# The opening of a two-layer graph network on one Trainium2 core: norms split, roundings reordered and low parts moved between engines in its first two steps

## The reference, cut to what matters

```
h  = relu(layernorm(x))
m  = Be * (H^T h)                 # Be = 1 / column counts
u  = H m ;  z = (u W1^T) * Dn + b1        # Dn = 1 / (H w), a guarded inverse
n  = layernorm(relu(z)) * gamma + beta
g  = Be * (H^T (n W2^T)) ;  x1 = x + h + Dn * (H g) + b2
xl = relu(layernorm(x1))
y2, y1, y0 = xl Wk[2], xl Wk[1], xl Wk[0];  s = xl (Wv a)      # scores
A  = adj * exp(leaky_relu(s_j + s_i)), rows divided by their sums
out = x1 + relu(y0 + A (y1 + A y2) + biases)
```

## Time and profile before

| | us |
|---|---|
| median of 3 runs (all: 831.15, 833.02, 833.21) | 833.02 |
| the profiled execution, its own time | 832.13 |
| its span, from the first to the last instruction | 830.3 |
| PE busy in it | 806.2 (97%) |
| DVE, ACT, POOL busy | 642.9 (77%), 474.0 (57%), 427.7 (52%) |
| chain that ended last, share of PE | 90% |
| issue to landing, median: x, adj_t, w_row | 4.6, 5.3, 3.3 |

### The profile page before, as it was taken

How to read it: one execution, slowest core, us unless ns; L and a number is a source line. 1 busy time by engine, 2 the same in 40 slices (tenths; PEclk the granted TensorE clock), 3 DMA queues, 4 the chain that set the end, 5 groups by cost and what they waited for, 6 DMA issues and landing times.

```text
span 830.3 us, 16639 instructions
## 1 busy us (share of the span) xinstructions
PE 806.2 (97%) x5750; PEld 752.3 (91%) x5750; DVE 642.9 (77%) x1728; ACT 474.0 (57%) x1004; POOL 427.7 (52%) x589
## 2 busy tenths in 40 slices
PE   7887999999999999999999999999999999999997
PEld 6876999999899998999999999999989999899986
DVE  6976887778887777887778788787888877777565
ACT  4335657384674828557483755738467473854654
POOL 4576363654826366382645737365472736632232
PEclk9998999999999999999999999999999999999999
DMA  9321204022040312204022030402204031110000
GB/s 299 119 65 52 89 1 153 15 77 89 0 164 0 110 54 66 98 0 164 0 76 88 26 138 0 150 14 76 88 0 164 0 122 43 52 51 1 26 24 29
DMA packets 39856, 57.83 MB, mean 70 GB/s; under 512 B 2576, under 2 KB 21008, under 8 KB 39824
## 3 DMA queue, kind: packets, MB, share of 16 engines
q1 hardware_dynamic: 39104, 57.42, 20.6%
q10 hardware_dynamic: 720, 0.01, 0.0%
HBM read 49.03 MB, written 8.39 MB: 69 GB/s over the span
## 4 chain that ended last, share of the span: by engine, by line
PE 90%; DVE 5%; POOL 2%; ACT 2%; issue 1%; ACTq 0%; POOLq 0%; DVEq 0%
PE ps L761 85%; PE ps L951 3%; PE ps L896 2%; PE ps L940 1%; POOL p_lo L476 1%; DVE st_r L1214 0%; DVE r_sb L1208 0%; POOL h_lo L392 0%; POOL y L406 0%; DVE st_x L1083 0%; POOL h_hi L387 0%; DVE part_b L1225 0%; DVE hw L1092 0%; DVE e_sb L1232 0%; DVE w_lo L1393 0%
## 5 line engine op out<-in xcount | busy, mean ns | idle before, releaser
L761 PE MATMUL ps<-w_hi,part_a 128*128 128x256 f32 (+1 forms) x512 | 156.3, 340 | 2.8 <-DVE part_a L1113 1.7
L406 POOL TENSOR_TENSOR y<-y,bk_row 128x256 f32<-128x256 f32 x64 | 56.3, 910 | 199.0 <-DVE a_lo L1238 199.0
L761 PE MATMUL ps<-w_lo,part_a 128*128 128x256 f32 (+1 forms) x384 | 122.6, 319 | 0.0
L761 PEld LDWEIGHTS ps<-w_hi,part_a 128*128 128x128 f32 x512 | 96.1, 188 | 15.9 <-DVE part_a L1113 2.6
L761 PE MATMUL ps<-wk_hi,xt_hi 128*128 128x258 f32 (+1 forms) x256 | 90.2, 352 | 5.3 <-DVE xt_lo L1138 4.9
L761 PE MATMUL ps<-wk_hi,xt_lo 128*128 128x258 f32 (+1 forms) x256 | 87.5, 342 | 0.0
L761 PE MATMUL ps<-wk_lo,xt_hi 128*128 128x258 f32 (+1 forms) x256 | 87.4, 341 | 0.0
L761 PEld LDWEIGHTS ps<-w_lo,part_a 128*128 128x128 f32 x384 | 72.7, 189 | 5.6
L1232 DVE TENSOR_TENSOR e_sb<-e_sb,adjt_sb 128x512 f32<-128x512 f32 x64 | 44.1, 690 | 43.3 <-ACT e_sb L631 43.3
L476 POOL TENSOR_TENSOR p_lo<-y,p_hi 128x256 fp32r<-128x256 f32 x64 | 45.5, 742 | 61.8 <-ACT p_hi L698 50.1
L462 POOL TENSOR_TENSOR xt_lo<-xl,xt_hi 128x256 fp32r<-128x256 f32 x60 | 57.1, 982 | 30.4 <-ACT xt_hi L704 30.4
(11 more groups left out here) (151 smaller groups left out, 2531.2 us busy)
## 6 DMA issues: line engine op xcount, KB each, us to landing
adj_sb<-in_adj SPq DMA_DIRECT2D x30, 512.0 KB, 5.7
adjt_sb<-in_adj_t SPq DMA_DIRECT2D x15, 1024.0 KB, 5.3
xin<-in_x SPq DMA_DIRECT2D x15, 512.0 KB, 4.6
out_dram<-x SPq DMA_DIRECT2D x15, 512.0 KB, 3.4
w_row<-in_adj SPq DMA_DIRECT2D x16, 256.0 KB, 3.3
adjt_sb<-in_adj_t SPq DMA_DIRECT2D x4, 256.0 KB, 6.6
e_sb<-in_w_t SPq DMA_DIRECT2D x2, 512.0 KB, 8.0
y<-in_wk SPq DMA_DIRECT2D x3, 256.0 KB, 7.4
```

What stands on the lines that cost most here:

```text
L406: pool.tensor_tensor(y10[:, t, D:], y10[:, t, D:], bk_row[:, :], ALU.add).then_inc(po_y0, 1)
L761: return pe.matmul(dst, stationary, moving, start=first, stop=last, skip_group_check=True)
```

## The change

It touches steps 0 and 1 alone:

- `w2_c` moves from `h_f` to the memory of `w1_f`, and its writer waits for `su_w1lo` in place of POOL's `po_skip`.
- POOL's `setup` starts after `dv_dn` (the end of the first `dn` chain) in place of `dv_inct`.
- In step 0, `h_lo` is made on DVE: after `g` tiles 0, 1 and 2, the last one ahead of `g` tile 3. POOL makes `h_hi` alone. The shift of x stands ahead of `y_lo(3)`.
- At the end of step 0 DVE runs the `dn` chain of step 1 and the four statistics of x ahead of and between; `u_lo(0)` and `u_lo(1)` of step 1 have only `stats_x1(0)` between them.
- In step 1 the norm is taken in two halves, x1's first and then x's: two aggregations, two powers on POOL, two shifts, and `x_of` waits for the first alone.
- In step 1 ACT and DVE have orders of their own: on ACT both `xt_of` stand directly behind `relu(1)`, and `h_of` is put between the `y2_of`; on DVE `lo_of_xt` stands ahead of the incidence tiles, these and `stats_r` stand between the rest, and the norm of r and `sums(0)` come behind `si` and `sj`.

```
-        w2_c = h_f
+        w2_c = e_sb[:, 0:TD, :].rearrange("p a (b n) -> p (a b) n", n=D)
...
+                elif s.k == 1:
+                    for lo_t, made in ((TI, 1), (0, 3)):
+                        part = slice(lo_t, lo_t + TI)
+                        wait(pool, dv_mvx, at(s, 1, made))
+                        pool.tensor_scalar(v_x[:, part], mv_x[:, part, 1], EPS_LN, 1.0, ALU.add,
+                                           ALU.mult).then_inc(po_vx, 2)
+                        wait(pool, po_vx, at(s, 1, made))
+                        pool.tensor_tensor(rs_x[:, part], v_x[:, part], minus_half[:, part],
+                                           ALU.pow).then_inc(po_rsx, 2)
...
                         h_hi_of(s, t)
-                        h_lo_of(s, t)
...
-                pool.wait_ge(dv_inct, TI)
+                pool.wait_ge(dv_dn, TI)
...
-                            wait(act, dv_nbx, at(s, 1))
+                            wait(act, dv_nbx, at(s, 1, 1 if s.k == 1 else 3))
...
+                def second_step_to_scores():
+
+                    for t in range(TI):
+                        x_of(t)
+                    relu(0)
+                    relu(1)
+                    xt_of(0)
+                    xt_of(1)
+                    relu(2)
+                    relu(3)
+                    for t in range(TI):
+                        y2_of(t)
+                        h_of(t)
...
                     z_tile(0)
                     z_tile(1)
                     dve.wait_ge(su_gam, 1)
-                    dve.wait_ge(po_skip, TI)
+                    dve.wait_ge(su_w1lo, TD)
...
                     y_lo(2)
+                    shift_of_x(0, TI)
                     y_lo(3)
-                    shift_of_x(0, TI)
                     incidence(3)
                     dve.wait_ge(su_c, 3)
-                    g_out()
+                    g_tile(0)
+                    h_lo_of(0)
+                    g_tile(1)
+                    h_lo_of(1)
+                    g_tile(2)
+                    h_lo_of(2)
+                    h_lo_of(3)
+                    g_tile(3)
...
                     sums(2)
                     sums(3)
+                    second = Step(4, 1, 1, NB)
+                    sign_of_total(second)
+                    stats_x(0, 2)
+                    safe_total(second)
+                    stats_x(1, 2)
+                    inverse_total(second)
+                    stats_x(2, 2)
+                    stats_x(3, 2)
                     for t in range(TI):
                         x1_tile(t)
-                    second = Step(4, 1, 1, NB)
+                    wait(dve, dv_x1, at(s, 0))
+                    dn_of_total(second)
                     u_lo(0, second)
-                    for t in range(TI):
+                    stats_x1(0)
+                    u_lo(1, second)
+                    for t in range(1, TI):
                         stats_x1(t)
-                    u_lo(1, second)
-                    for t in range(TI):
-                        stats_x(t, 2)
...
+                def second_step_to_y2():
+
+                    dve.wait_ge(dv_st1, at(s, -1))
+                    dve.memset(landed_0[:, :], 0.0)
+                    for t in range(TI, 2 * TI):
+                        last = dve.bn_aggr(mv_x[:, t, :], st_x[:, t, :])
+                    last.then_inc(dv_mvx, 2)
+                    for t in range(TI):
+                        last = dve.bn_aggr(mv_x[:, t, :], st_x[:, t, :])
+                    last.then_inc(dv_mvx, 2)
                     z_tile(0)
+                    shift_of_part(slice(TI, 2 * TI), 1)
                     z_tile(1)
+                    stats_r(0)
+                    z_tile(2)
+                    shift_of_part(slice(0, TI), 3)
+                    z_tile(3)
+                    lo_of_xt(0)
+                    lo_of_xt(1)
                     incidence(0)
+                    stats_r(1)
+                    lo_of_y2(0)
+                    stats_r(2)
+                    lo_of_y2(1)
                     incidence(1)
+                    lo_of_y2(2)
+                    stats_r(3)
+                    lo_of_y2(3)
...
+                if s.k == 1:
+                    for _ in norm_r():
+                        pass
+                    sums(0)
```

More of the change, by code:

```diff
@@ L578, in y2_of @@
                         act.activation(y2_hi[:, t, 0:D], ps0[:, (t + 2) % 4, 0:D], ACT.Copy).then_inc(ac_y2, 1)
[L580 to L591, removed]
-                else:
-                    act.wait_ge(su_w2, 1)
-                    act.activation(w2_hi[:, :, :], w2_c[:, :, :], ACT.Copy).then_inc(su_w2hi, 1)
@@ L595, in step @@
[L595 to L606, removed]
@@ new lines, in to_scores @@
+                def to_scores():
+                    x_of(0)
+                    x_of(1)
+                    x_of(2)
+                    x_of(3)
+                    if s.k != 0:
+                        h_of(0)
+                    relu(0)
+                    if s.k != 0:
+                        h_of(1)
+                    relu(1)
+                    if s.k != 0:
+                        h_of(2)
+                    else:
+                        act.wait_ge(su_w2, 1)
+                        act.activation(w2_hi[:, :, :], w2_c[:, :, :], ACT.Copy).then_inc(su_w2hi, 1)
+                    relu(2)
+                    xt_of(0)
+                    relu(3)
+                    xt_of(1)
+                    if s.k == 0:
+                        act.wait_ge(su_pe, 1)
+                        act.activation(c_e[:, :], ps1[:, 2, 0:1], ACT.Identity, bias=ab_c[:, :]).then_inc(su_c, 1)
+                        act.activation(c0_row[:, :], ps1[:, 0, 0:D], ACT.Copy).then_inc(su_c, 1)
+                        act.activation(wk_f[:, :, D:D2], ps1[:, 1, 0:2 * TD].rearrange("p (a b) -> p a b", a=TD),
+                                       ACT.Copy).then_inc(su_wk, 1)
+                        act.wait_ge(su_c, 1)
+                        act.activation(c_e[:, :], ps1[:, 2, 1:2], ACT.Identity, bias=c_e[:, :]).then_inc(su_c, 1)
+                    if s.k != 0:
+                        h_of(3)
+                    relu_v(0)
+                    relu_v(1)
+                    y2_of(0)
+                    y2_of(1)
+                    relu_v(2)
+                    y2_of(2)
+                    relu_v(3)
+                    y2_of(3)
@@ L617, in spread @@
+                if s.k == 1:
+                    second_step_to_scores()
+                else:
+                    to_scores()
                 def spread(t):
@@ L1294, in p_out, with g_tile @@
                         p_tile(t)
+                def g_tile(t):
+                    wait(dve, pe_g, at(s, 0, t))
+                    dve.scalar_tensor_tensor(g_f[:, t, :], ps1[:, (t + 1) % 4, 0:D], be[:, q, t:t + 1],
+                                             c0_row[:, :], ALU.mult, ALU.add).then_inc(dv_g, 1)
                 def g_out():
@@ L1299, in g_out @@
                     for t in range(TI):
-                        wait(dve, pe_g, at(s, 0, t))
-                        dve.scalar_tensor_tensor(g_f[:, t, :], ps1[:, (t + 1) % 4, 0:D], be[:, q, t:t + 1],
-                                                 c0_row[:, :], ALU.mult, ALU.add).then_inc(dv_g, 1)
+                        g_tile(t)
                 def inct_of():
@@ L1344, in x1_out, with h_lo_of @@
                         var_of_x1(1)
-                def first_loads():
[L1348 to L1352, removed]
+                def h_lo_of(t):
+                    wait(dve, ac_hf, at(s, 1, t))
+                    wait(dve, h_hi_made, at(s, 1, t))
+                    dve.tensor_tensor(h_lo[:, t, :], h_f[:, t, :], f32(h_hi[:, t, 0:D]),
+                                      ALU.subtract).then_inc(h_lo_made, 1)
+                def first_loads():
                     def inct_tile(t):
@@ L1469, in step @@
                 chain = iter(())
-                if s.next or s.here:
+                if s.here or s.next:
                     chain = norm_x()
@@ L1523, in opening_of_second, with shift_of_part, to_y2 @@
+                    lo_of_y2(1)
                     incidence(1)
-                    sums(0)
+                    lo_of_y2(2)
+                    stats_r(3)
+                    lo_of_y2(3)
+                def shift_of_part(part, made):
+                    wait(dve, po_rsx, at(s, 1, made))
+                    dve.scalar_tensor_tensor(nb_x[:, part], mv_x[:, part, 0], -1.0, rs_x[:, part],
+                                             ALU.mult, ALU.mult).then_inc(dv_nbx, 2)
+                def to_y2():
+                    opening_of_steps()
+                    stats_r(0)
+                    z_tile(2)
+                    stats_r(1)
+                    z_tile(3)
+                    stats_r(2)
+                    lo_of_xt(0)
+                    stats_r(3)
+                    if s.here:
+                        for _ in norm_r():
+                            pass
```

(11 more changed lines are left out.)

20 lines of the change are left out of this document (4 added, 16 removed).

## The result

The changed kernel takes 827.87 us (median of 6 runs, 827.17 to 828.16) against 833.18 before (6 runs beside it, 831.15 to 833.37). The ratio is 0.9939, 95% interval 0.9927 to 0.9952: 0.5 to 0.7% faster. Sent again, unaltered, it took 828.17 (826.46 to 829.47) against 832.19, ratio 0.9952 (0.9937 to 0.9967). The profiled execution took 827.77, with a span of 826.0, 4.3 less than that of before.

The account below looks back on a forecast made before the run. PE bounds the kernel, without gaps worth naming from about 83 us, so only earlier waits can be won. The parts move the transposes of si from 79.30 to 73.95; 832.6 less 5.4 gives 827.2, range 825.0 to 830.2.

Parts of the forecast that it names:

- Part 1: POOL's setup behind the first dn chain: PE's products 0.4 late, y stage 0.15 later; bounds 0.3 earlier to 2.8 later.
- rival (b): Setup reaches su_rows at 32.9, y stage and all behind up to 2.6 later; gain about 2.8, 829.8; chance 0.08.
- Part 2: Step 0, h_lo on DVE: PE's m stage starts 2.2 us earlier than 48.0; low bound 1.5, at most 3.0.
- Part 3: End of step 0: DVE's chain lets PE reach the second half of z tile 0 at 59.55, gain 1.5 us.
- Part 4: Step 1, split norm and new orders: x_of at 62.95, 3.0 earlier transposes of xl, y2 at 68.75, 4.2 earlier.
- The clock: PE's clock stays up despite new gaps, so y2 and y10's first tile, 6.3 before, shrink by 1.9.
- rival (a): The clock still falls, y2 runs at the lower level and 1.9 is not won; gain 3.5, 829.1; chance 0.16.
- A clock below 1 between 66 and 76: Listed sign that the forecast is wrong: PE's granted clock under 1.00 in that stretch around y2.
- The wait for si: Step 1, behind y2: PE ready at 73.15, DVE later at 73.7, transposes of si at 73.95.
- Rival (d): Idle time only moves: DVE's chain is as long as before and PE waits elsewhere; 832.5; chance 0.04.
- (e): Slower: each of POOL's setup additions locked out at 1.73, su_rows at 38.7, 8.6 late; 835.8; chance 0.02.
- (c): DVE isn't the later one from the end of step 0 on, mark at PE's own 72.3; gain 7.0, 825.6; chance 0.12.

Follow-up runs that it names:

- e8: Changed kernel plus nine unread unit-matrix products on PE between the transposes of xl and y2 in step 1; 828.06 us, ratio to before 0.9939.
- e6: Changed kernel with step 1's norm taken over all eight tiles at once, other orders as changed; 829.25 us, ratio to before 0.9958.
- c1: The changed kernel sent once more, unaltered; 828.17 us, ratio to before 0.9952.
- e3: Changed kernel plus thirty unread unit-matrix products on PE between the transposes of xl and y2 in step 1; 831.63 us, ratio to before 0.9993.
- e5: Changed kernel with step 1 in the orders of the kernel before, steps -1 and 0 as changed; 833.71 us, ratio to before 1.001.
- e2: Changed kernel with the row that PE waits for made first in POOL's setup; 825.09 us, ratio to before 0.9908.
- e4: Changed kernel with step 0's h_lo back on POOL and g_out in one piece on DVE; 829.68 us, ratio to before 0.9967.
- e9: Changed kernel with the row first in setup and nine unread unit-matrix products before y2; 823.94 us, ratio to before 0.990.
- e1: Changed kernel with POOL's setup starting after dv_inct again, all else as changed; 825.75 us, ratio to before 0.9916.
- e10: As e9, plus six more unread unit-matrix products behind the first m stage (step -1), before u; 824.01 us.

## Why the prediction was right

The forecast was 827.2 and a gain of 5.35 at the mark; measured are 827.87 and 4.66 at the mark in the profiled execution (5.3 between the medians of the first runs, 4.0 in the repeat). The sum came out near, and that is in part luck: none of its five stretches is exact, and the errors have both signs:

| stretch | before | after | gain | forecast |
|---|---|---|---|---|
| start to second part of g | 41.65 | 42.54 | -0.9 | -0.15 |
| to m | 6.35 | 4.26 | 2.1 | 2.35 |
| to the transposes of xl | 20.05 | 18.51 | 1.5 | 0.75 |
| to y2 | 4.93 | 3.32 | 1.6 | 1.3 |
| to the transposes of si | 6.32 | 6.01 | 0.3 | 1.1 |

- **Part 1, the setup.** "PE's products come 0.4 late" (by its own sum, 30.6 less 30.07, it was 0.5): they came 0.66 late by the clock of the trace, but 2.0 late against PE, which was ready at 28.8 and not at 30.07. The row's time was met only by errors that cancel: setup started at 23.02 and not 23.95, its additions took 0.70 each and not 0.74, and its last step took 2.10 and not 0.72. The two starts belong together. The first profile of the changed kernel had the clock up in `u`, where the one of before had it at 0.50 from 16 to 19, so PE and the `dn` chain were both early. e8's execution had the same fall as before, with PE ready at 30.3, and the row came at 32.22: there too PE waited 1.95, and its products came 2.15 late. So the wait isn't from the earlier PE. The term that was mis-sized is the row, 1.4 too low: DVE's `w_lo` of 1.24 and the incidence tiles ran then, and POOL was locked out. That was rival (b)'s mechanism, in one instruction instead of eight; it had a chance of 0.08. Behind the wait came a fall of the clock, which no case of mine priced there. It can be priced from the row to `m`: 15.70 in e6, whose clock stayed up (30.97 to 46.67), 16.07 with it down for 3.6 (changed), and 17.6 to 17.7 with it down for 7 (c1, e3, e5, e8). So it costs 0.4 to 2.0, and the -0.9 of the table's first row is from one of the quicker executions in this stretch: in the eight with this wait the second part of `g` starts from 42.41 to 45.57, in four of them at 44.2 to 44.3. e2 shows the size of the whole: 2.5 at `m` (2.4 against e6), 2.8 to 3.1 in the median.
- **Part 2, h's low parts.** 2.35 against 2.1 measured. The mechanism holds, with a split that the working didn't give: e4 has 0.9 for DVE, and the rest stays in e4, where the earlier shift is the likely cause of 0.8. One `h_lo` met POOL and took 0.94, not 0.5.
- **Part 3, the end of step 0.** Low by half, in two small terms (forecast 0.75, measured 1.5). DVE's last `g` tile started 0.2 ahead of `m`, not 0.1 behind it, and its chain from there to `u_lo(1)` took 12.54 (46.58 to 59.12), not 12.95: the dn chain and the statistics of x are 1.6 (54.68 to 56.28), not 2.0. The two sums beside POOL (1.9) and m_parts (3.2) were as priced.
- **Part 4, the second step.** The orders did what was said: `x_of` at 63.18 (62.95), y2 at 68.63 (68.75), PE's wait for `xl` 0.3 (0.5). e6 and e5 give 1.15 to the split norm and 1.76 to the orders, of 3.15 between `m` and y2.
- **The clock** was the step that failed. I took it that it stays up. It fell at y2 in the profiled execution (rival (a), chance 0.16) and stayed up in the repeat; over all kernels with this gap of 2.2 it fell in six profiled executions of seven. "A clock below 1 between 66 and 76" was also one of the signs of being wrong that the prediction named. The 1.9 for a fall as long as that of before is right (6.32 less 4.5 with the clock up), but a fall can be longer: with the clock down all through the stretch takes 7.2 to 7.3, 2.7 to 2.8 more.
- **The wait for si**, forecast at 0.8, isn't there: of DVE's two incidence tiles each took some 0.35, not 0.6. The first ran while POOL was idle (67.1 to 70.6, it waits for `h_of(0)`, which ends at 70.5), the second at 71.35, just as POOL ended an addition; POOL's `h_hi` behind it took 0.59 in place of 0.41. In e9, with the clock up, PE goes on at 70.54 to 70.59, straight behind DVE's copy of `si` (70.34, 0.15).

The sum landed near because parts 3 and 4 gained 1.1 more than forecast, and the setup and `g` 1.0 less. What is missing, 0.7, is at y2, where the fall cost 1.5 (6.01 against 4.51) and the wait for `si` of 0.8 didn't come. The mechanisms of parts 2 to 4 were right; that 827.2 was met to 0.7 with the row late and the clock falling twice is in part luck. Rival (d), nothing gained, and (e) are out. (c) is out as well: PE still waits for DVE in part 3 (0.55) and at y2 (2.2). e9 gains more than (c) had, 8.7 at the mark, but by other means, the row and the fillers.

## What to carry to other kernels

Moving a block of POOL's work to a later place keeps it from slowing DVE at one place, but everything in the block moves along, and can be slowed at the new one: look for the one instruction in it that a third engine waits for, and put it first (2.4 us here, for one row). Measure between marks inside the trace when single executions spread by more than the edit is worth, and price a gap of PE with the clock: at y2 a stall of 2 us could cost up to 2.8 more behind it. Where a gap can't be closed, a few unread products that just fill it cost nothing that the runs could tell. With the other gap closed, they went with a spread of 0.23 us in place of 2.6; with that gap open (e8) they brought nothing. Too many delay what stands behind them (e3).

## What the runs showed of the hardware

- The clock can fall while PE is at work: in the changed kernel PE stood from 28.8 to 30.7, was busy again, and the level fell to 1.2 GHz at 32.3. Seven of the eight profiled executions with this wait had a fall between 30 and 33, none of the four without it (e1, e2, e9, e10). At y2, behind gaps of 2.2, it fell in six executions of seven; behind gaps of 3.8 in both. In the four with fillers there (e3, e8, e9, e10) it didn't. The Trainium skill (TensorE: Matmul & The Clock Gate, "HAM oscillation") says that waits between bursts of matmuls bring the lower clock. The runs agree with that; they also show that work behind the wait doesn't prevent it, and that the same code has it one time and not the next.
- VectorE and GpSimd hold each other up, in both directions. The row of 0.72 took 2.10 beside DVE's subtraction of 1.24 and the incidence tiles; in e2, with POOL's additions beside them, the two tiles took 1.82 and not 0.85. The z tiles, which read one operand from PSUM, weren't slowed: in the changed kernel one took 0.73 beside POOL's addition (66.42) and the next 0.74 with POOL idle (67.14).
- A product of the 128 x 128 unit matrix in fp32 is two records of 0.114 us on PE: 60 of them took 6.86.
